# A recommendation tower on one core: the last gathers paced by TensorE's progress, three single table rounds first, and a different loop order in the batch copies

## What is computed

```python
e = jnp.stack([tbl_0[ids[:, 0]], ..., tbl_25[ids[:, 25]]], axis=1)      # 512 x 26 x 128
all_vecs = concatenate([r_dense_proj[:, None, :], e], axis=1)           # 27 vectors a sample
interactions = einsum('bnd,bmd->bnm', all_vecs, all_vecs)               # a 27x27 gram a sample
z = concatenate([dense, interactions[:, rows, cols]], axis=1)           # upper triangle, 351 pairs
h = maximum(concatenate([z, dense], axis=1) @ W_top1 + b_top1, 0)       # 607 -> 512
h = maximum(h @ W_top2 + b_top2, 0)                                     # 512 -> 256
y = h @ W_top3                                                          # 256 -> 1
```

## Time and profile before

| | |
|---|---|
| median of 3 runs | 140.96 us (140.27 to 141.63) |
| the profiled execution | 141.28 us |
| its span, from first to last instruction | 139.5 us |
| mean granted TensorE clock in it | 0.902 of full |
| busy: PE, DVE, POOL, ACT | 108.0, 82.8, 70.7, 51.2 us |
| DMA | 16.49 MB, mean 118 GB/s |

### The profile page before, as it was taken

The page is one execution under the profiler, slowest core; times in us unless marked ns, Lnnn a source line. Parts: engine busy times, 40 slices in busy tenths (PEclk is TensorE's granted clock), DMA queues, the critical chain, the costliest instruction groups (busy, mean ns, idle before and its releaser), DMA issues.

```text
span 139.5 us, 3355 instructions
## 1 busy us (share of the span) xinstructions
PE 108.0 (77%) x1416; PEld 83.7 (60%) x1416; DVE 82.8 (59%) x173; ACT 51.2 (37%) x86; POOL 70.7 (51%) x60
## 2 busy tenths in 40 slices
PE   0079299999999999989985422279999995995971
PEld 0057188778888888867743311267588684683560
DVE  5286396999999999979989100055035266014101
ACT  3040561794949678089160000012042131040130
POOL 4787788888888888888888777200000000000000
PEclk9999959999999999999997555555799999999999
DMA  2999999999999999981111112100000000000000
GB/s 65 236 281 239 303 237 262 234 244 240 239 247 236 285 275 220 230 260 50 38 38 42 51 44 56 38 7 5 0 5 5 5 5 0 0 5 5 0 0 3
DMA packets 7677, 16.49 MB, mean 118 GB/s; under 512 B 2007, under 2 KB 2648, under 8 KB 7662
## 3 DMA queue, kind: packets, MB, share of 16 engines
q1 hardware_dynamic: 5998, 12.87, 37.6%
q0 software_dynamic: 1664, 3.41, 9.9%
HBM read 16.27 MB, written 0.00 MB: 117 GB/s over the span
## 4 chain that ended last, share of the span: by engine, by line
PE 40%; DVE 23%; issue 16%; DMA 12%; ACT 4%; SPq 1%; another core or an unknown queue 1%; POOL 0%; DVEq 0%; POOLq 0%
DVE hot L422 14%; DMA tab_raw<-in_tbl 12%; PE gram_ps L543 12%; DVE tab_lo L426 6%; PE fill_ps L595 6%; PE l_ps L566 4%; PE fill_ps L507 3%; PE fill_ps L509 3%; ACT vec L233 2%; PE l_ps L569 2%; PE l_ps L573 2%; PE fill_ps L529 2%; PE l_ps L570 2%; PE turn_ps L581 2%; DVE vec L412 2%
## 5 line engine op out<-in xcount | busy, mean ns | idle before, releaser
L327 POOL DMA_INDIRECT gathered<-in_tbl,ids_sb x52 | 69.8, 1343 | 16.6 <-issue 14.9
L507 PE MATMUL fill_ps<-hot,tab_hi 125*128 125x512 f32 x112 | 47.1, 420 | 8.8 <-issue 8.3
L509 PE MATMUL fill_ps<-hot,tab_lo 125*128 125x512 f32 x112 | 45.9, 410 | 0.0
L422 DVE TENSOR_SCALAR hot<-ids_bc,row_id 125x1024 fp32r<-125x1024 int32 (+1 forms) x60 | 42.8, 714 | 3.3 <-DMA ids_bc<-in_ids_t 2.1
L507 PEld LDWEIGHTS fill_ps<-hot,tab_hi 125*128 125x128 f32 x112 | 22.6, 202 | 14.9 <-issue 9.0
L543 PE MATMUL gram_ps<-vec 128*32 128x27 f32 x1024 | 17.5, 208 | 13.8 <-issue 13.8
L344 ACT CAST tab_hi<-tab_raw 125x512 fp32r<-125x512 f32 (+1 forms) x30 | 17.9, 610 | 25.8 <-DMA tab_raw<-in_tbl 16.6
L426 DVE TENSOR_TENSOR tab_lo<-tab_raw,tab_hi 125x256 fp32r<-125x256 f32 (+1 forms) x60 | 24.0, 400 | 5.4 <-issue 4.4
L543 PEld LDWEIGHTS gram_ps<-vec 128*32 128x32 f32 x1024 | 14.3, 123 | 18.8 <-issue 18.8
L509 PEld LDWEIGHTS fill_ps<-hot,tab_lo 125*128 125x128 f32 x112 | 22.5, 201 | 4.4
L459 DVE COPY_PREDICATED pairs<-second,gram_ps 128x104 f32<-128x104 int32 x16 | 4.4, 274 | 31.3 <-ACT pairs L383 31.1
(11 more groups left out here) (46 smaller groups left out, 61.5 us busy)
## 6 DMA issues: line engine op xcount, KB each, us to landing
tab_raw<-in_tbl SPq DMA_DIRECT2D x8, 448.0 KB
ids_bc<-in_ids_t SPq DMA_DIRECT2D x13, 256.0 KB
tab_raw<-in_tbl SPq DMA_DIRECT2D x4, 560.0 KB
gathered<-in_tbl,ids_sb POOLq DMA_INDIRECT x52
w_raw<-in_w_pairs SPq DMA_DIRECT2D x3, 256.0 KB
w_sb<-in_W_top SPq DMA_DIRECT2D x1, 512.0 KB
tab_raw<-in_tbl SPq DMA_DIRECT2D x2, 224.0 KB
tab_raw<-in_tbl SPq DMA_DIRECT2D x8, 52.0 KB
```

The lines of the kernel that those rows point to most:

```text
L327: pool.indirect_dma_start(out=gathered[:, n % GSLOTS, j, :], out_offset=None, in_=tables[f], in_offset=bass.IndirectOffsetOnAxis(ap=ids_sb ...
L422: nc.vector.tensor_scalar(hot[0:HP, (PIECE * c + k) % HOTS, 0:n, :], ids_bc[0:HP, slot, 0:n, :], row_id[0:HP, j:j + 1], None, ALU.is_equal ...
L507: nc.tensor.matmul(into, tab_hi[0:HP, c % PSLOTS, f, k * D:(k + 1) * D], one_hot, start=first, stop=False)
L509: used = nc.tensor.matmul(into, tab_lo[0:HP, c % PSLOTS, f, k * D:(k + 1) * D], one_hot, start=False, stop=last)
```

## The change

Four edits are made together.

1. **POOL waits.** `AFTER_GRAM` and `AFTER_L1` name 11 of the last 16 gathers by (tile, batch, table in the batch). Each of them waits until PE has finished so many gram units (`gram_made`) or so many l1 layers (`l1_made`). The five between them follow the one ahead.
2. **Rounds.** The pair (3, 6) becomes two rounds of one table, so there are 8 rounds, the first three single. The order of steps is written anew: `dense` comes behind the third round, `batch(2, 2)` moves behind the last hot round and `batch(2, 3)` further back into the tail.
3. **First half table.** The two DMAs with the first half of the first table (table 2) are issued by ScalarE, ahead of its table load, and no longer by SP. `dense` is loaded behind three rounds of tables, as before behind three tables.
4. **Batch copies.** In `fill_copy` the loop over the 3 or 4 tables becomes the innermost one. In `vec` the vectors of one sample are neighbours, so a copy now writes runs of 3 or 4 floats, where each float went 32 floats away from the one before. The work is the same.

PE's wait for `ident_made` moves to its start.

```diff
-ROUNDS = [[2], [3, 6], [7, 8], [19, 21], [23, 25], [0, 4], [5, 12]]
-NK = [8, 8, 8, 8, 8, 10, 10]
+ROUNDS = [[2], [3], [6], [7, 8], [19, 21], [23, 25], [0, 4], [5, 12]]
+NK = [8, 8, 8, 8, 8, 8, 10, 10]
...
-    out += hot(6) + batch(2, 1) + batch(2, 2) + gram(0, 0, 1, 2, 3)
-    out += gram(1, 0) + batch(2, 3) + [("turn", 0)] + gram(1, 1) + [("l1", 0)] + gram(1, 2) + [("h1t", 0)]
-    out += gram(1, 3) + [("l2", 0)] + gram(2, 0) + [("turn", 1)] + batch(3, 0) + gram(2, 1)
+    out += hot(7) + batch(2, 1) + gram(0, 0, 1, 2, 3)
+    out += gram(1, 0) + batch(2, 2) + [("turn", 0)] + gram(1, 1) + [("l1", 0)] + gram(1, 2) + [("h1t", 0)]
+    out += batch(2, 3) + gram(1, 3) + [("l2", 0)] + gram(2, 0) + [("turn", 1)] + batch(3, 0) + gram(2, 1)
...
+AFTER_GRAM = {(2, 3, 0): 1, (2, 3, 1): 2, (2, 3, 2): 4, (3, 0, 0): 5, (3, 0, 1): 6, (3, 1, 0): 7, (3, 1, 2): 8,
+              (3, 2, 1): 10, (3, 3, 1): 11}
+AFTER_L1 = {(3, 0, 3): 1, (3, 2, 2): 2}
...
-            return copy(vec[:, step[1], :, first:first + n].rearrange("p (g s) n -> p n g s", s=S),
-                        src[:, 0:n * P].rearrange("p (n s g) -> p n g s", n=n, s=S))
+            return copy(vec[:, step[1], :, first:first + n].rearrange("p (g s) n -> p g s n", s=S),
+                        src[:, 0:n * P].rearrange("p (n s g) -> p g s n", n=n, s=S))
...
-            load_tables(0)
-            load_tables(1)
-            sp.dma_start(dense[:], ins["r_dense_proj"].rearrange("(q t) d -> q t d", t=TILES)) \
-                .then_inc(dense_landed, 16)
-            for r in range(2, NR):
+            for r in range(NR):
                 load_tables(r)
+                if r == TSLOTS - 1:
+                    sp.dma_start(dense[:], ins["r_dense_proj"].rearrange("(q t) d -> q t d", t=TILES)) \
+                        .then_inc(dense_landed, 16)
...
                     for j, f in enumerate(BATCHES[i]):
+                        if (t, i, j) in AFTER_GRAM:
+                            pool.wait_ge(gram_made, AFTER_GRAM[t, i, j])
+                        if (t, i, j) in AFTER_L1:
+                            pool.wait_ge(l1_made, AFTER_L1[t, i, j])
                         pool.indirect_dma_start(
...
         def _(act):
+            half = NK[0] // 2 * D
+            for a, b in ((0, 112), (112, HP)):
+                act.dma_start(tab_raw[a:b, 0, 0, 0:half],
+                              tables[ONEHOT[0]].rearrange("(p k) d -> p (k d)", p=HP)[a:b, 0:half]) \
+                    .then_inc(first_half_landed, 16)
```

More of the change, by code:

```diff
@@ L78, in hot @@
         return [("hot", r)]
-    out = hot(0) + [("dense",)] + hot(1) + batch(0, 0) + batch(0, 1) + hot(2) + batch(0, 2) + batch(0, 3)
-    out += hot(3) + batch(1, 0) + batch(1, 1) + hot(4) + batch(1, 2) + hot(5) + batch(1, 3) + batch(2, 0)
-    out += hot(6) + batch(2, 1) + batch(2, 2) + gram(0, 0, 1, 2, 3)
-    out += gram(1, 0) + batch(2, 3) + [("turn", 0)] + gram(1, 1) + [("l1", 0)] + gram(1, 2) + [("h1t", 0)]
-    out += gram(1, 3) + [("l2", 0)] + gram(2, 0) + [("turn", 1)] + batch(3, 0) + gram(2, 1)
+    out = hot(0) + hot(1) + batch(0, 0) + hot(2) + [("dense",)] + batch(0, 1) + hot(3) + batch(0, 2) + batch(0, 3)
+    out += hot(4) + batch(1, 0) + hot(5) + batch(1, 1) + batch(1, 2) + hot(6) + batch(1, 3) + batch(2, 0)
+    out += hot(7) + batch(2, 1) + gram(0, 0, 1, 2, 3)
+    out += gram(1, 0) + batch(2, 2) + [("turn", 0)] + gram(1, 1) + [("l1", 0)] + gram(1, 2) + [("h1t", 0)]
+    out += batch(2, 3) + gram(1, 3) + [("l2", 0)] + gram(2, 0) + [("turn", 1)] + batch(3, 0) + gram(2, 1)
     out += [("l1", 1)] + gram(2, 2) + [("h1t", 1)] + batch(3, 1) + gram(2, 3) + [("l2", 1)] + batch(3, 2)
@@ L281, in load_tables @@
                     src = tables[f].rearrange("(p k) d -> p (k d)", p=HP)
-                    halves = [(0, NK[r] * D, table_landed[slot])]
-                    if r == 0:
-                        m = NK[0] // 2 * D
-                        halves = [(0, m, first_half_landed), (m, 2 * m, table_landed[slot])]
-                    for m, n, landed in halves:
-                        for a, b in ((0, 112), (112, HP)):
-                            sp.dma_start(tab_raw[a:b, slot, k, m:n], src[a:b, m:n]).then_inc(landed, 16)
-            sp.dma_start(ids_sb[:], ins["ids"].rearrange("(q t) f -> q t f", t=TILES)).then_inc(ids_landed, 16)
-            load_tables(0)
-            load_tables(1)
-            sp.dma_start(dense[:], ins["r_dense_proj"].rearrange("(q t) d -> q t d", t=TILES)) \
-                .then_inc(dense_landed, 16)
-            for r in range(2, NR):
+                    first = NK[0] // 2 * D if r == 0 else 0
+                    for a, b in ((0, 112), (112, HP)):
+                        sp.dma_start(tab_raw[a:b, slot, k, first:NK[r] * D], src[a:b, first:]) \
+                            .then_inc(table_landed[slot], 16)
+            sp.dma_start(ids_sb[:], ins["ids"].rearrange("(q t) f -> q t f", t=TILES)).then_inc(ids_landed, 16)
+            for r in range(NR):
                 load_tables(r)
+                if r == TSLOTS - 1:
+                    sp.dma_start(dense[:], ins["r_dense_proj"].rearrange("(q t) d -> q t d", t=TILES)) \
+                        .then_inc(dense_landed, 16)
                 if r == NR - 2:
@@ L489, in _ @@
         def _(pe):
+            pe.wait_ge(ident_made, 1)
             for step in STEPS:
@@ L520, in _ @@
                     if kind == "dense":
-                        pe.wait_ge(ident_made, 1)
                         pe.wait_ge(dense_landed, 16)
```

## The result

The changed kernel takes 147.73 us (median of 4 runs, 147.38 to 148.77) where the kernel before took 140.62 on the same chip in the same session (140.07 to 141.63): ratio 1.0509, 95% interval 1.0426 to 1.0593. It is slower by 7 us; 131.0 was predicted. Medians here are of all runs, while ratios are formed from the undisturbed runs of both kernels, so a ratio need not be the quotient of two medians.

The account below looks back on a forecast made before the run. It took DMA to bound the first half and instruction supply, starved by gathers, to lose time from 73 to 106 us; 122.0 plus 7.8 for gathers gave 129.8 span, forecast as 131.0 us, range 122.5 to 139.

Parts of the forecast that it names:

- Rounds and the order at the start: 0.4 us gained: Hot stage: last tables still land at 59.9 us, DVE ends at 70, first gram unit at 73.0 instead of 73.36.
- PE is fed its instructions by DMA, and while gathers are in flight they come in drips: Gram units: gathers in flight slow PE's instruction supply, explaining 13.8 us of waits for "issue" before the change.
- rival A: Gram units: a 7 us pause fills PE's store, so no unit starves; 123.5, or 122.5 with sooner start; chance 0.22.
- What the 16 gathers of the new tail cost: Gram stage: five gathers at 1.25 us, the others free, plus 1.5 us for lower clock; 7.8 us in all.
- Tail with PE never short of instructions: From the first gram unit to the end: 13.9 + 2.4 + 32.7 us after a start at 73.0, ending at 122.0.
- Half a table by ACT: 0: Start of the kernel: ScalarE issuing half the first table gains 0 us, since the landing at 59.9 decides.
- batch copies: 0.6 gained: Batch copies with contiguous writes: 0.3 us less each, two on the path before gram(3, 0), so 0.6 us gained.
- B: Gram units: gathers starve PE as before, seven costing 2.84 us each, 19.9 in all; 145 us measured; chance 0.11.
- C: Gram units: the dripping has nothing to do with gathers, so 19.3 us stay lost; 140 to 142 us; chance 0.05.
- D: End of tail: last gathers come late, batch (3, 3) waits and seven gathers cost 1.75 to 2 each; 136; chance 0.12.

Follow-up runs that it names:

- `rounds_only`: Kernel before with only the new rounds, three of them single, and the new order of steps, without the waits: 146.98 us, ratio 1.0599.
- `late_spaced`: Kernel before with three GpSimd memsets after each gather from the tenth batch on: 128.97 us where before took 127.97.
- `plain_tile3`: Kernel before with tile 3's 13 gathers replaced by plain SyncE DMAs of rows 0 to 127: 126.84 us where before took 127.66.
- the spaced kernels: Versions of the kernel before and the changed kernel with useless GpSimd memsets after gathers to space them out: 128.97 to 145.94 us in quick sessions.
- `plain_tile3_again`: Kernel before with tile 3's 13 gathers as plain SyncE DMAs of rows 0 to 127, in a slow session: 133.39 us where before took 139.64.
- `half_by_act`: Kernel before with only half of the first table issued by ScalarE: 140.41 us, ratio 1.012.
- `waits_only`: Kernel before with only the eleven waits of gathers for gram units and l1 layers: 144.63 us, ratio 1.0442.

## Why the prediction was wrong

*The step that failed is "Rounds and the order at the start: 0.4 us gained".* It argued that the last tables land at 59.9 whatever the order, "so DVE ends its last round at 70 us again". In the slow session the last tables were issued at 54.2 us, not 42.7, their last packet started at 64.8, and DVE ended at 80.3; the first unit started at 83.73, not 73.0. The step took it that each engine sees PE's counts at once, and they came up to 16.6 us late. `rounds_only` shows that this edit alone does it: 146.98 where before took 138.55. Its bounds ran from 1 us sooner to 0.8 later, from the nearest rows that I had, but no row with "remote" was weighed, although the kernel before had them: 1.2 us of DVE and 2.1 of ACT in the hot stage, 6.7 of ACT beside the gram units. In the quick session the step failed to the other side: last tables issued at 40.0 us, first unit at 69.28, where kernels with the old order and an undisturbed start had 74.15 (`late_spaced`) and 75.37 (`plain_tile3`). The landing at 59.9 was no fixed point in either case, since SyncE can issue a round only when `hot` frees a slot.

*Why this order meets so much more of it is argued, not shown.* The new order has three single rounds with 512-wide `hot` tiles at the start. PE runs level with DVE, so each piece is needed again soon, and a count that is late by 10 us stops everything at once. Beside 512-wide work or an idle DVE a gather takes 0.95 us, beside 1024-wide work up to 1.69, so while the stage hangs the gathers follow each other fastest. What the late counts are, and why GpSimd's work goes with them in some sessions only, stays open; the spaced kernels that should have told it fell on quick sessions. In the three slow traces with the new order and no spacing, the last late count came 3.2 to 3.5 us after GpSimd's 20th gather, when GpSimd itself stood waiting for PE.

*"PE is fed its instructions by DMA, and while gathers are in flight they come in drips".* That the drip goes with gathers was right in slow sessions: with 13 plain DMAs in their place it is gone, and the total is 6.2 us less. That it is the fetching of instructions nothing bears out. The 11 packets of the instruction queue took 0.9 to 1.4 us each in the trace of before, of 16 KiB each, and none was moved between 75.8 and 91.6 us, where most of the drip lies. The 1.04 us at 93.98, which the prediction took for one more wait of the drip, is another thing: the same matmul, the 307th of the gram stage, waits 1.04 us in the quick session and 1.24 in `plain_tile3_again`, with no gather on GpSimd. Its cause stays open, and it was no argument against rival A.

*One cause of the drip and the late counts?* The drip shows in the nine slow traces that have gathers beside the gram units, and in no quick one. Late counts show in slow traces alone, but in very different size: 11.6 and 16.6 us in the changed kernel, 1.6 in the kernel before, none for VectorE's `hot` in `half_by_act`, whose gram count reached ACT 9.1 us late instead. All ten slow traces list fewer updates of `piece_used` than were made. Yet they miss updates of other origin too (in the kernel before 149 of DVE's 169 are listed, and 937 of 1680 of the DMAs' landings), where the quick traces list every engine's and 1586 to 1635 of the 1680. So one cause is likely, but the missing updates don't place it on PE's side.

*"What the 16 gathers of the new tail cost", 7.8 us.* 61.9 us in the slow session less 54.0 in the quick one, for the same kernel, is 7.9 us, of which idle time for "issue" is 5.6 (7.4 less 1.8). The sum was right there, and 0 in a quick session, with 17 gathers. The places were nearly those I gave: the gathers at 94.7 and 95.9, beside l1 0, cost nothing, and those at 97.9, 100.3, 101.6, 113.1 and 114.4 drip. But (3, 2, 2) and (3, 3, 0), the last two of these, were to find the supply filled, and (3, 3, 1) and (3, 3, 2), at 116.5 and 117.7, were to be free, and all four drip. So it is in part luck that the sum agrees.

*"Tail with PE never short of instructions", to 122.0 us.* From the first unit it allowed 49.0 us; the quick session shows 54.0. The first third was mis-sized: 20.0 us from the first unit to turn 1 instead of 16.3; from turn 1 on it took 34.0 for 32.7. The nine gram units were put at 0.69 us each, 6.2 in all. That is a misreading of the earlier trace rows, whose 0.69 is for 50 matmuls, while a unit has 64. The same unit in the timeline of the kernel before:

```profile
110.89 0.76 PE L543 MATMUL gram_ps<-vec 128*32 128x27 f32 x64
```

In the quick session the nine took 9.1 us (1.81 for the first two, 3.3 for the next three, then 1.08, 0.91, 1.02 and 1.01), with a granted clock of 0.66 from 72.83 to 75.70 and 0.50 from there to 80 us, after the 1.7 us for which PE waited for DVE:

```profile
72.83 2.89 PE L554 MATMUL gram_ps<-vec 128*32 128x27 f32 x178 [1.74 <-DVE pairs L470]
76.77 0.42 PE L554 MATMUL gram_ps<-vec 128*32 128x27 f32 x14 [1.04 <-issue]
```

That wait was foreseen: the third unit starts 3.3 us after the first in the slow session and 3.55 in the quick one, for 3.8.

*What edit 1 was worth.* In a slow session the wait table pins 16 gathers to the gram stage whatever went before. Before paid its late counts back there (66.1 us after an early start, 57.0 after a late one, sums 139.5 and 136.7); with the waits nothing is paid back. That fits `waits_only`: 77.9 and 64.3, 6 us above before, though nothing in its hot stage was changed.

*Half a table by ACT: 0* and *batch copies: 0.6 gained.* Both came out slightly above before (1.012 and 1.0066), so the copies' 0.6 was not there, though their durations are those forecast.

*The rivals.* B's number, 145, is nearest, but not its mechanism: the loss lies ahead of the gram units, which gained 4.3 us. Against C stands `plain_tile3_again`, where the drip goes with the gathers. Of D's wait for batch (3, 3) there is nothing: PE starts its transposes at 122.51 us with no idle time before them. A, by which gathers cost the units nothing, describes the quick sessions, which nobody foresaw; there the kernel before had nothing to win back either.

## What to carry to other kernels

A gap whose releaser the profile calls "remote" on a single core is a row to be weighed, even if it costs 1 or 2 us so far: here it grew to 12 in a kernel that waits on the same counts more tightly. Don't pin work to a stage if its place was what paid delays back. More buffers ahead of the engine that waits for another's count would be the next thing to try where gathers by GpSimd run beside it; no run here did. And time the kernel before in every session: a change that costs 5% in one cost nothing in another.

## What the runs showed of the hardware

- The same program took 138.55, 139.64 and 140.62 us (medians) in three sessions and 127.66, 127.97 and 127.67 in three others; single runs of it went up to 148.94 in the first session, and none of a slow session was as short as any of a quick one.
- In slow sessions TensorE's updates of `piece_used` reached their waiters up to 16.6 us after the matmul, in the same traces 0.04 to 0.09 us at other times, while TensorE started 0.15 us after VectorE's work in the very hole; the trace lists 18 to 23 updates for the 23 or 26 made. In the ten quick traces all are listed, each under 0.02 us after its matmul.
- In slow sessions matmuls of gram units came 4 to 6 per 0.75 us while GpSimd worked on a gather, and the units waited 6.3 to 13.8 us for "issue" in a kernel; with ordinary DMAs of the same bytes it was 2.8, and 1.8 to 4.0 in quick sessions.
- A gather of 128 rows kept GpSimd for 0.95 us with 0.30 between two, and for 1.69 beside 1024-wide work of VectorE.
- A copy of 384 floats from PSUM took 557 ns on VectorE and 547 on ScalarE with the batch's values side by side in the destination, 808 and 948 with them scattered.
